# Convolution of 20 of 32 heads as three F32R passes with split Toeplitz tiles and split products

## What is computed

```python
kv = jnp.einsum('bhil,bhjl->bijhl', k_, v_)          # products of channels i, j
y = jnp.fft.irfft(jnp.fft.rfft(kv, n=fft_size) * jnp.fft.rfft(ssm_kernel, n=fft_size), n=fft_size)[..., :L]
out = y + kv * D[None, None, None, :, None]
out = jnp.einsum('bijhl,bhil->bjhl', out, q_)
```

## Time and profile before

| | us |
|---|---|
| median of 3 runs | 1978.05 |
| range of these | 1978.04 to 1983.03 |
| the profiled execution: time | 1980.6 |
| its span in the trace | 1978.8 |
| mean granted TensorE clock | 0.97 of 2.4 GHz |

### The profile page before, as it was taken

How to read it: one execution, slowest core, us unless ns; L and a number is a source line. 1 busy time by engine, 2 the same in 40 slices (tenths; PEclk the granted TensorE clock), 3 DMA queues, 4 the chain that set the end, 5 groups by cost and what they waited for, 6 DMA issues and landing times. The chain is left out here.

```text
span 1978.8 us, 33002 instructions
## 1 busy us (share of the span) xinstructions
PE 1801.7 (91%) x12272; PEld 1480.8 (75%) x12272; DVE 1240.9 (63%) x2286; ACT 929.9 (47%) x2388; POOL 300.3 (15%) x377
## 2 busy tenths in 40 slices
PE   7999999999996999999999996799998689999985
PEld 6889998988984878888888885577776455555554
DVE  4654444444447656555555634788888578888866
ACT  2333333333334443333333222666666488888843
POOL 0000000000012111111111000233334221212011
PEclk9999999999999999999999998999999799999998
DMA  4320000000014221111101013001101667665512
GB/s 162 107 65 1 22 22 23 22 22 22 1 54 133 86 75 44 36 30 43 49 17 38 12 43 128 11 1 46 52 23 43 152 167 167 165 171 127 144 43 85
DMA packets 83581, 131.42 MB, mean 66 GB/s; under 512 B 9344, under 2 KB 25344, under 8 KB 83424
## 3 DMA queue, kind: packets, MB, share of 16 engines
q1 hardware_dynamic: 83424, 129.33, 23.1%
HBM read 75.21 MB, written 20.53 MB: 48 GB/s over the span
## 5 line engine op out<-in xcount | busy, mean ns | idle before, releaser
L2263 ACT ACTIVATE e_p<-e_s_ps,e_nb 128x512 f32<-128x512 f32 x256 | 175.6, 701 | 32.4 <-DVE e_nb L2327 31.7
L2327 DVE TENSOR_REDUCE e_nb<-e_s_ps 128x2 f32<-128x1024 f32 x128 | 155.7, 1217 | 44.6 <-PE e_s_ps L2422 44.5
L1703 ACT ACTIVATE p<-p,nb,rq 128x128 f32<-128x128 f32 (+1 forms) x256 | 136.9, 541 | 93.1 <-DVE nb L1804 93.1
L887 PE MATMUL yp<-ccy,toep 128*128 128x288 f32 x600 | 158.0, 411 | 5.4 <-ACT ccy L869 3.6
L2432 PE MATMUL e_t_ps<-ident,e_p 128*128 128x128 f32 x1024 | 142.9, 277 | 20.5 <-DVE e_pT L2334 12.7
L2432 PEld LDWEIGHTS e_t_ps<-ident,e_p 128*128 128x128 f32 x1024 | 115.3, 142 | 56.7 <-issue 48.1
L1224 DVE SCALAR_TENSOR_TENSOR hm<-gu_ps,us_col,sg 128x256 f32<-128x256 f32 x88 | 42.3, 481 | 179.6 <-ACT sg L1113 179.6
L80 PE MATMUL q_ps<-a_xt_hi,wq_hi 128*128 128x256 f32 x512 | 149.1, 291 | 0.0
L472 ACT ACTIVATE ex<-ex 128x512 f32<-128x512 f32 x64 | 40.4, 632 | 221.9 <-DVE ex L565 221.9
L82 PE MATMUL q_ps<-a_xt_hi,wq_lo 128*128 128x256 f32 x512 | 144.3, 282 | 0.0
L81 PE MATMUL q_ps<-a_xt_lo,wq_hi 128*128 128x256 f32 x512 | 143.9, 281 | 0.0
(11 more groups left out here) (339 smaller groups left out, 5139.5 us busy)
## 6 DMA issues: line engine op xcount, KB each, us to landing
x_after<-n_r SPq DMA_DIRECT2D x23, 512.0 KB, 3.0
toep<-padded_kernels SPq DMA_DIRECT2D x32, 256.0 KB, 3.6
qs<-e_xh SPq DMA_DIRECT2D x64, 128.0 KB, 2.6
qs<-e_xl SPq DMA_DIRECT2D x64, 128.0 KB, 2.6
ks<-e_ch SPq DMA_DIRECT2D x64, 128.0 KB, 2.6
ks<-e_cl SPq DMA_DIRECT2D x64, 128.0 KB, 2.6
x<-in_x SPq DMA_DIRECT2D x8, 512.0 KB, 4.0
a_x<-in_x SPq DMA_DIRECT2D x8, 512.0 KB, 4.2
```

The lines of the kernel that those rows point to most:

```text
L887: last = pe.matmul(yp[:, lo % 2, 0:NCOL], self.toep[h % 2][:, (lo - li) * P:(lo - li + 1) * P], self.ccy(h)[:, li, 0:NCOL], start=(li == 0 ...
L1703: act.activation(p[n % 3][:, h, part[t]], p[n % 3][:, h, part[t]], ACT.Exp, bias=nb[i][:, t, h:h + 1], scale=rq[u][:, t:t + 1], accum_out= ...
L2263: act.activation(pr[i][:, a, :], s_ps[i][:, a, :], ACT.Exp, bias=nb[i][:, a:a + 1], accum_out=sums[t][:, j, q:q + 1]).then_inc(e_done, 1)
L2327: dve.tensor_reduce(nb[i][:], s_ps[i][:], AX.X, ALU.max, negate=True).then_inc(nb_done, 1)
```

## The change

For heads 12 to 31 a unit takes three F32R passes in place of each fp32 product. `l0_front` rounds the kernels and stores a high and a low version beside the fp32 one. `windows` loads two tiles for these heads, `toep_hi` (two buffers) and `toep_lo` (two buffers at the start of the weight ring, which is free by then). The products get a high part `c_hi`, rounded by ACT in two halves, for which there is **one buffer**, and a low part `c_lo` (two buffers), subtracted by POOL. The even unit also waits until both low halves are there. Heads 0 to 11 stay as they were.

```diff
@@ l0_front @@
+                    if v == 5:
+                        sp.wait_ge(klo_done, 1)
+                        for part, dst in ((khi, padded[1]), (klo, padded[2])):
+                            sp.dma_start(dst[:, PAD:PAD + D], part.bitcast(F32)).then_inc(pad_stored, 16)
+                            sp.dma_start(dst[:, 0:PAD], kpad[:, 0:PAD]).then_inc(pad_stored, 16)
...
+                    if b == 2:
+                        act.wait_ge(pad_added, 1)
+                        act.activation(khi, kpad[:, PAD:PAD + D], ACT.Copy).then_inc(khi_done, 1)
...
+                    if b == 2:
+                        dve.wait_ge(khi_done, 1)
+                        dve.tensor_tensor(klo, kpad[:, PAD:PAD + D], khi, ALU.subtract).then_inc(klo_done, 1)
@@ Convolution @@
     def windows(self, sp, h):
-        row = self.padded[h:h + 1, 1:1 + D]
         if h >= 2:
             sp.wait_ge(self.conv_mm, 2 * h - 2)
-        sp.dma_start(self.toep[h % 2][:], bass.AP(tensor=row.tensor, offset=row.offset, ap=[[1, P], [1, D]]))\
-          .then_inc(self.toep_loaded[h % 2], 16)
+        k = h % 2
+        for place, rows_of in ([(self.toep[k], self.padded[0])] if h < HF else
+                               [(self.toep_hi[k], self.padded[1]), (self.toep_lo[k], self.padded[2])]):
+            row = rows_of[h:h + 1, 1:1 + D]
+            sp.dma_start(place[:].bitcast(F32), bass.AP(tensor=row.tensor, offset=row.offset, ap=[[1, P], [1, D]]))\
+              .then_inc(self.toep_loaded[k], 16)
...
+    def round_products(self, act, h, half):
+        li = slice(2, 4) if half == 0 else slice(0, 2)
+        act.wait_ge(self.cc_done, h + 1)
+        act.wait_ge(self.sq_done, h + 1)
+        act.wait_ge(self.conv_mm, 2 * h - 1 + half)
+        act.activation(self.c_hi[:, li, :], self.ccy(h)[:, li, 0:NCOL], ACT.Copy).then_inc(self.chi_done, 1)
+
+    def lower_products(self, pool, h):
+        for half, li in ((0, slice(2, 4)), (1, slice(0, 2))):
+            pool.wait_ge(self.chi_done, 2 * (h - HF) + half + 1)
+            pool.tensor_tensor(self.c_lo[h % 2][:, li, 0:NCOL], self.ccy(h)[:, li, 0:NCOL], self.c_hi[:, li, :],
+                               ALU.subtract).then_inc(self.clo_done, 1)
...
+            if h >= HF:
+                pe.wait_ge(self.clo_done, 2 * (h - HF) + 2)
+        if h >= HF:
+            for lo in (2 - 2 * half, 3 - 2 * half):
+                for li in range(lo + 1):
+                    cols = slice((lo - li) * P, (lo - li + 1) * P)
+                    last = three_pass(pe, yp[:, lo % 2, 0:NCOL], self.toep_hi[h % 2][:, cols], self.toep_lo[h % 2][:, cols],
+                                      self.c_hi[:, li, :], self.c_lo[h % 2][:, li, 0:NCOL], li == 0, li == lo)
@@ l0_mixer, POOL @@
                         cv.products(pool, heads_at(t))
+                        if heads_at(t) >= HF:
+                            cv.lower_products(pool, heads_at(t))
@@ l0_mixer, ACT @@
-                    if heads_at(t):
+                    if heads_at(t) and (first or heads_at(t) < HF):
                         cv.squares(act, heads_at(t))
...
                         if t is not None:
-                            conv(t)
+                            conv(t, True)
...
+                    h = heads_at(t) if t is not None else None
+                    h = h if h and h >= HF else None
                     if m is not None:
                         silu(m, j)
+                    if h and j != 0:
+                        cv.squares(act, h)
+                    if h:
+                        cv.round_products(act, h, 0)
+                    if m is not None:
                         round_h(m, j)
+                    if h:
+                        cv.round_products(act, h, 1)
```

More of the change, by code:

```diff
@@ L35, in __init__ @@
         self.x0 = ctx.enter_context(nc.sbuf_tensor("x0", [P, T, D], F32))
+        self.ring_at = -(-nc.sbuf_base // 32) * 32
         self.ring = ctx.enter_context(nc.sbuf_tensor("ring", [P, RING], F32))
@@ L338, in l0_front @@
         th, tl = sb("th", [P, 2, S], F32R), sb("tl", [P, 2, S], F32R)
+        khi, klo = [part[0:HC].rearrange("p h n -> p (h n)") for part in (th, tl)]
         pad_place = sb("kpad", [HC, PAD + D + 1])
@@ L354, in l0_front @@
         v_done, kv_done = core.sem("v_done"), core.sem("kv_done")
-        pad_zeroed, pad_loaded, pad_added, pad_stored = (core.sem(f"kpad_{n}") for n in (
-            "zeroed", "loaded", "added", "stored"))
+        pad_zeroed, pad_loaded, pad_added, pad_stored, khi_done, klo_done = (core.sem(f"kpad_{n}") for n in (
+            "zeroed", "loaded", "added", "stored", "hi", "lo"))
         bq_loaded, bq1_set = core.sem("bq_loaded"), core.sem("bq1_set")
@@ L394, in _ @@
                         sp.wait_ge(pad_added, 1)
-                        sp.dma_start(padded, kpad).then_inc(pad_stored, 16)
+                        sp.dma_start(padded[0], kpad).then_inc(pad_stored, 16)
+                    if v == 5:
[3 more added lines that the diff above has]
+                            sp.dma_start(dst[:, 0:PAD], kpad[:, 0:PAD]).then_inc(pad_stored, 16)
                     if v >= 4:
@@ L398, in _ @@
                 split.load(sp, 2 * B - 1)
-                sp.wait_ge(pad_stored, 16)
+                sp.wait_ge(pad_stored, 80)
                 def body(b, u, first, last):
@@ L464, in round_t @@
                     act.wait_ge(t_mm, n + 1)
+                    if n == 0:
+                        act.wait_ge(pad_stored, 80)
                     wait_from(act, o_mm, n)
@@ L761 @@
 SHARED = 2 * 4 * KT * H0 * HD
+HF = 12
 class Convolution:
@@ L786, in __init__ @@
         self.early = [take(f"ccy{k}", [P, LB, XCOL]) for k in (2, 3)]
+        at = core.nc.alloc_sbuf_tensor_at
+        self.c_lo = [at(f"cc_lo{k}", [P, LB, XCOL], F32R, offset=place[0] + 4 * LB * XCOL * k) for k in range(2)]
         self.steady = [take(f"ccy{k}", [P, LB, XCOL]) for k in range(2)]
         self.ct = take("ct", [P, LB, 2, 2, HB])
+        self.toep_hi = [at(f"toep_hi{k}", [P, D], F32R, offset=place[0] + 4 * D * k) for k in range(2)]
+        self.toep_lo = [at(f"toep_lo{k}", [P, D], F32R, offset=core.ring_at + 4 * D * k) for k in range(2)]
         self.toep = [take(f"toep{k}", [P, D]) for k in range(2)]
@@ L804, in __init__ @@
         self.c_turned, self.c_copied, self.cc_done, self.sq_done = s("c_turned"), s("c_copied"), s("cc_done"), s("sq_done")
+        self.chi_done, self.clo_done = s("chi_done"), s("clo_done")
         self.conv_mm, self.ys_done, self.ot_done = s("conv_mm"), s("ys_done"), s("ot_done")
@@ L883, in unit @@
             pe.wait_ge(self.sq_done, h + 1)
-            pe.wait_ge(self.toep_loaded[h % 2], 16 * (h // 2) + 16)
+            self.wait_windows(pe, h)
+            if h >= HF:
[6 more added lines that the diff above has]
+                                      self.c_hi[:, li, :], self.c_lo[h % 2][:, li, 0:NCOL], li == 0, li == lo)
+            last.then_inc(self.conv_mm, 1)
+            return
         for lo in (2 - 2 * half, 3 - 2 * half):
@@ L970, in l0_mixer @@
         ot, xh = cv.ot, cv.xh
+        cv.c_hi = sb("cc_hi", [P, LB, NCOL], F32R)
         st2, mv2, rstd2 = sb("m_st2", [P, 6]), sb("m_mv2", [P, 2]), sb("m_rstd2", [P, 1])
@@ L1040, in _ @@
                     if t is not None and t % 2 == 0 and t // 2 + 1 < HC:
+                        if t // 2 + 1 == HF:
+                            sp.wait_ge(split.lo_done, len(split.pieces))
                         cv.windows(sp, t // 2 + 1)
@@ L1052, in _ @@
                     sp.wait_ge(stored[(NB - 2 - k) % 3], 32 * ((NB - 2 - k) // 3 + 1))
+                sp.wait_ge(cv.conv_mm, NU)
                 after.load_weights(sp)
@@ L1120, in round_h, with conv @@
                     act.activation(hh[n % 2][:], hm[:], ACT.Copy).then_inc(hh_done, 1)
-                def conv(t):
+                def conv(t, first=False):
                     if t % 4 == 0 and t // 4 < HC // 2:
@@ L2828, in decoder @@
         between = [nc.dram_tensor(f"x_after_{i}", (B * S, D), F32, kind="Internal").ap() for i in range(1, 6)]
-        padded = nc.dram_tensor("padded_kernels", (HC, PAD + D), F32, kind="Internal").ap()
+        padded = [nc.dram_tensor(f"padded_kernels{n}", (HC, PAD + D), F32, kind="Internal").ap()
+                  for n in ("", "_hi", "_lo")]
         to_kv = Ahead(core, "a1", x, kv_weights(wkT, wvT), 2 * D)
```

2 lines of the change are left out of this document (added).

## The result

The changed kernel takes 1995.83 us, median of five runs (1991.98 to 1998.25), against 1978.58 for the kernel before in as many: a ratio of the means of 1.0082, 95% interval 1.0071 to 1.0094. It is slower by 17.3 us by the medians and by 16.2 by the ratio, where 22.8 were forecast. Its profiled execution took 1995.83 us with a span of 1993.8, 15.0 above the span of before.

What follows compares the result with a forecast made beforehand. PE was taken to bound the fused stage, within 1.3 us a block; -17.7 + 1.3 + 1.3 + 22.0 + 4.4 + 11.5 = +22.8 gave 2000.9 us for the median, range of 8 in 10 1984 to 2016.

Steps and rivals of the forecast that it cites:

- What PE saves: Units of the 20 changed heads: passes of 0.132 us save 0.88 a head, 17.7 us in all.
- The odd units of slot 0: Five shorter odd units in slot 0 only lengthen PE's wait for `m_xt_lo`: 5 x 0.26 = 1.3 us lost.
- The gap in slot 1: Ahead of slot 1's even unit PE waits 4.4 us for POOL's `cc_lo`, five times: 22.0 us lost (19.5 to 26.5).
- How the two subtractions and `hl` bear each other: In slots 0 and 1, POOL's subtractions and DVE's `hl` take turns by whole instructions; gap 4.4 us, without turns 3.9.
- Slots 3 and 4: Slot 3's odd unit hides in slot 4's DMA wait, 1.3 us; slot 4's even unit is late, 4.4 (0 to 6).
- The power and the copies of `yp` behind the subtractions: Copies of slot 4's even unit end some 0.3 us before slot 5's odd unit wants `yp`: this just holds.
- The clock: Half-clock stretch behind each of slot 1's five gaps, 2.3 us lost each: 11.5 us (0 to 15).
- the rest costs nothing: Kernel rounding and four small DMAs in `l0_front`, the second Toeplitz tile and the wait before the next weights cost nothing.
- The low parts are there in time: Rival, chance 0.12: PE finds `c_lo` ready in slot 0, no gap, no fall of the clock; -15.1 us, 1963.
- The clock stays: Rival, chance 0.17: the gaps come but the clock does not fall; +11.3 us, 1989 (1984 to 1994).

Runs made afterwards that it cites:

- the filled kernel: Changed kernel plus matmuls of 256 columns into `yp` ahead of the waits of slot 1's five even units: 1990.55 us, ratio 1.0061 to the kernel before.
- the last kernels: Changed kernel, slot 0's work begun in slot 10, first rounding behind `silu(10)` and `round_h(10)`: 1966.76 us with slot 3's sums moved into slot 2 too, 1969.70 without.
- the same early start: Changed kernel, slot 0's sums, products, squares and first rounding begun in slot 10, slot 3's sums in slot 2: 1.0029 or 0.9943 by the rounding's place.
- slot 0 alone: Against the kernel before, only the five heads whose work starts in slot 0 (15, 19, 23, 27, 31) get F32R passes: 2009.16 us, ratio 1.0142.
- the shorter chain: Changed kernel with slot 0's two roundings on ACT ahead of the context's copy and `silu`: 1989.18 us, ratio 1.0049 to the kernel before.
- slot 3 alone: Against the kernel before, only the five heads whose work starts in slot 3 (12, 16, 20, 24, 28) get F32R passes: 1981.88 us, ratio 1.0007.

## Why the prediction was right, step by step

**What PE saves**, right: 0.132 us a pass was taken, 0.132 measured, so 17.7 us. The rule of the Trainium skill ("TensorE: Matmul & The Clock Gate", section "Back-to-back issue gap"), which it calls that of a single isolated matmul, gave 0.1225; the rows of the changed kernel bear the measurement out.

**The odd units of slot 0**, right: the wait for `m_xt_lo` is 1.09 where it was 0.84, five times 0.25 to 0.27, 1.3 us as in the sum.

**The gap in slot 1**, right in place, releaser and count, a little off in size. From `gate_up(m, 0)` to the unit it is 10.01, 10.01, 9.99 and 10.00 us, against 882.31 - 876.56 = 5.75: 4.26, 4.26, 4.24 and 4.25 lost, where 4.4 were in the sum. In the last block it is 8.68, a loss of 2.93. There ACT has no copy of the context to do, since the last head's context is already in place; the changed kernel's ACT in that block:

```profile
1110.41 0.48 ACT L1170 ACTIVATE sg<-gu_ps,gs_col 128x256 f32<-128x256 f32 x1 [0.23 <-PE gu_ps L83]
1112.11 0.69 ACT L857 ACTIVATE cc_hi<-ccy 128x576 fp32r<-128x576 f32 x1 [1.22 <-POOL ccy L885]
```

The step "five times" took the block shown for all five. The sum was 22.0, measured 19.9.

**How the two subtractions and `hl` bear each other**, right in the order, off in what it costs POOL. `hl` lasts 1.33 us where it lasted 0.43, as forecast (1.4), and `terms` 2.15 instead of 0.95. The changed kernel's POOL, the two subtractions one by one:

```profile
812.05 1.40 POOL L862 TENSOR_TENSOR cc_lo<-ccy,cc_hi 128x576 fp32r<-128x576 f32 x1 [2.12 <-ACT cc_hi L857]
813.41 1.58 POOL L862 TENSOR_TENSOR cc_lo<-ccy,cc_hi 128x576 fp32r<-128x576 f32 x1
```

`hl` ends at 813.73, 0.28 us behind the first, and `terms` at 815.80, 0.81 behind the second: they end in turn, subtraction, `hl`, subtraction, `terms`. But I had POOL's second subtraction wait for the whole 0.43 of `hl`, and it lasted only 0.18 longer than the first; the two took 2.94 us together. The Trainium skill ("SBUF — State Buffer", section "Who interferes with whom") has the exclusion; the rows agree in that neither operation of DVE ends before the subtraction that it met. The loss comes out 0.15 below the 4.4 and above the 3.9 without turns.

**Slots 3 and 4**, right in kind, too high: in the sum 1.3 + 4.4. PE waits for the DMA, then for `cc_lo`; the changed kernel's PE in two blocks (answers to the earlier trace rows):

```profile
835.57 0.66 PE L1381 MATMUL m_tr_ps<-ident,m_x 128*128 128x128 f32 x4 [0.43 <-DMA m_x<-x_after]
837.14 0.37 PE L81 MATMUL yp<-cc_hi,toep_hi 128*128 128x288 f32 x1 [0.90 <-POOL cc_lo L862]
```

```profile
911.51 0.66 PE L1381 MATMUL m_tr_ps<-ident,x 128*128 128x128 f32 x4 [1.12 <-DMA x<-x_after]
912.40 0.38 PE L81 MATMUL yp<-cc_hi,toep_hi 128*128 128x288 f32 x1 [0.23 <-POOL cc_lo L862]
```

The two cover each other: 1.33 us together in one, 1.35 in the other. The waits for `cc_lo` come to 3.6 us, 0.2 to 1.1 each where 1 to 2 were forecast, and the DMA waits to 2.8 against 3.2 before. What they cost is a little more, since a unit that waited also starts some 0.17 us further behind the turn than the idle time tells. From the last pass of `gate_up` ahead of the turn to the unit it is 2.02, 2.28, 2.29, 2.28 and 2.28 us, against 0.91, 0.99, 1.09, 3.18 and 1.01 before: 4.0 lost instead of 5.7. The rows for the second of these, the kernel before and the changed kernel (whose unit, at 837.14, is shown above):

```profile
828.80 0.28 PE L82 MATMUL gu_ps<-m_xt_hi,wu_lo 128*128 128x256 f32 x1
...
829.79 3.56 PE L887 MATMUL yp<-ccy,toep 128*128 128x288 f32 x14
```

```profile
834.86 0.28 PE L83 MATMUL gu_ps<-m_xt_hi,wu_lo 128*128 128x256 f32 x1
```

The long DMA wait of 2.40 did not come in the changed kernel, which is why the block 956.80 to 1032.03 is only 1.7 us longer than its counterpart of 73.5. The power and the copies of `yp` behind the subtractions held: no unit of slot 5 waits.

**The clock**, right in kind, the term furthest off: 11.5 in the sum, 7.1 by the filled kernel. The step that was wrong is a stretch behind each of the five gaps, at a mean of the two in the rows. There was none behind the 2.77 of the last block. Of the four others one was long (6.8 us, cost 2.7) and three short (3.4 us, cost 1.5 each); the mean of 2.3 gave the long one too much weight. So the clock over a block is 0.96 to 0.98, where about 0.95 was forecast.

**The sum by what was measured**: -17.7 + 1.3 + 19.9 + 4.0 + 7.1 = +14.6 in the stage. The three terms that were off, by 2.1, 1.7 and 4.4, were all too high; none made up for another. The stage grew by 430.74 - 415.53 = 15.2 us (735.13 to 1165.87 against 733.92 to 1149.45), so 0.6 us of it are not placed. The trace ahead of the stage is 1.2 longer and what follows 1.4 shorter. Neither was traced to the change. The other kernels of the study start the stage at 734.5 to 737.1, all of them later than the 733.92 of before. That is 0.6 to 3 us which the forecast took at nothing ("the rest costs nothing"), and it stays open whether the four small DMAs and the rounding of the kernels are in it.

**The rivals.** "The low parts are there in time" named the right place and the right condition, roundings 4.4 us earlier than slot 0 allows; the last kernels made that condition true and came to 1966.8, against the 1963 given for it. "The clock stays" is what the filled kernel shows, 1990.6 against 1989.

## What to carry to other kernels

A cheaper product on the bound engine pays only where its extra inputs are ready; ask of each place what the side engine does just before it, not how busy it is. Here ACT at 48% and POOL at 18% cost more than the bound engine won. When a piece of work is moved ahead in a queue, put it behind the work that the bound engine waits for next: the same early start gave 1.0029 with the rounding ahead of `silu(10)` and 0.9943 with it behind. And a gap on TensorE can cost more than its length: those of 2.4 to 4.1 us here mostly had a slow stretch behind them, and for the four of 4.1 us, where the filled kernel priced it, that cost another 1.5 to 2.7 us.

## What the runs showed of the hardware

**Gaps of 2.4 to 2.8 us are undecided.** The same gap is followed by half clock or not, from block to block: 2.58 or 2.59 us two times in five, 2.77 not and 2.76 (slot 0 alone) so, 2.43 for a DMA so and 2.40 not, 2.44 to 2.47 nine times in ten. The gap of 2.73 or 2.74 us ahead of the last `gate_up(m, 0)` (1149.45) stands in all eleven kernels, and in nine of the profiled executions a slow stretch follows it. All eight gaps of 4.07 to 4.09 had a slow stretch. The Trainium skill ("TensorE: Matmul & The Clock Gate", section "Part 1: The HAM clock gate") says that where the clock changes isn't tied to the kernel's own start and so differs from run to run. No run here shows that by itself; the windows of the shorter chain agree in so far as equal gaps within one run end differently. The gap of 2.73 us in the kernel with slot 3 alone, with a window behind it, at full clock where the earlier trace rows has 0.50:

```profile
1151.57 0.38 PE L81 MATMUL gu_ps<-m_xt_hi,wg_hi 128*128 128x256 f32 x1 [2.73 <-DVE m_xt_lo L1283]
```

```profile
1152.80:1156.00 3.20, 3.20 (x29) 3.20 (x29) 0.48 (x1) 0.75 (x2) 0.00 (x0) 1.00 0.00 0
```

The window of the last block in the changed kernel, and of its counterpart with slot 0 alone, behind 2.77 and 2.76 us:

```profile
1115.96:1119.36 3.40, 3.40 (x26) 3.40 (x27) 2.88 (x4) 0.78 (x3) 0.00 (x0) 1.00 0.03 7
```

```profile
1128.00:1131.40 3.40, 3.32 (x15) 3.35 (x16) 2.88 (x4) 0.42 (x1) 0.00 (x0) 0.53 0.01 2
```

**DVE and POOL finish in turn, and DVE pays for it.** Beside two subtractions of POOL in a row, `hl` lasted 1.33 us and `terms` 2.15, which is 0.90 and 1.20 more than without, while POOL's second subtraction lasted 1.58 against 1.40 for its first.
